# A fused attention layer: the tensor engine's program written out, two tiles moved between the sums, output buffers per chunk, and one PSUM bank moved from row scores to transposed scores

## The reference

```
xn = layernorm(x)                              # x: 2 x 2048 x 1024
q, k, v = xn @ wq, xn @ wk, xn @ wv            # 32 query heads, 8 key/value heads, width 32
scores = where(causal, q k^T * 32**-0.5, min)  # four query heads share one key/value head
s = (softmax(scores) @ v) @ wo
base = xn @ W_base.T + b_base
lora = sum over the top 2 of 8 experts of w_e * (xn @ A_e^T) @ B_e^T * 2
out = x + s * silu(base + lora)
```

## Time and profile before

| | |
|---|---|
| time, median of 3 runs | 3578.84 us (3575.22 to 3588.54) |
| the profiled execution: its own time / its span | 3588.89 us / 3587.1 us |
| PE busy, in all | 3328.6 us, 93% of the span |
| stretch of `attend` in which all five engines run | about 720 to 2820 us |
| mean granted clock of PE | 0.957 |

### The profile page before, as it was taken

How to read it: one execution, slowest core, us unless ns; L and a number is a source line. 1 busy time by engine, 2 the same in 40 slices (tenths; PEclk the granted TensorE clock), 3 DMA queues, 4 the chain that set the end, 5 groups by cost and what they waited for, 6 DMA issues and landing times. The chain is left out here.

```text
span 3587.1 us, 59110 instructions
## 1 busy us (share of the span) xinstructions
PE 3328.6 (93%) x17920; PEld 2219.9 (62%) x17920; DVE 1889.7 (53%) x4622; ACT 1443.8 (40%) x2658; POOL 1371.6 (38%) x565
## 2 busy tenths in 40 slices
PE   6999999799989988989999998999999699999999
PEld 5888888554545544544554554554554488877887
DVE  5333332676666666766766666676673222223333
ACT  3122121165655555655655555565565210100100
POOL 0000000075665665766766675676577100000000
PEclk9999999699999999999999999999999899999999
DMA  6555544356556556656656655655565454435554
GB/s 223 160 163 180 160 153 135 89 125 130 128 122 135 126 119 138 135 122 133 141 119 136 135 125 121 139 130 121 130 153 130 138 172 137 133 126 190 193 190 172
DMA packets 285847, 511.84 MB, mean 143 GB/s; under 512 B 41120, under 2 KB 156832, under 8 KB 263584
## 3 DMA queue, kind: packets, MB, share of 16 engines
q1 hardware_dynamic: 260256, 333.04, 31.5%
q0 software_dynamic: 23040, 167.78, 23.2%
q10 hardware_dynamic: 2304, 7.87, 0.6%
HBM read 205.03 MB, written 134.74 MB: 95 GB/s over the span
## 5 line engine op out<-in xcount | busy, mean ns | idle before, releaser
L890 POOL TENSOR_TENSOR added<-added,probs 128x2048 f32<-128x2048 f32 (+3 forms) x320 | 1182.5, 3695 | 806.8 <-PE o_ps L961 772.5
L1067 DVE TENSOR_REDUCE row_max<-rows_ps 128x1 f32<-128x512 f32 x1536 | 996.3, 683 | 417.6 <-PE rows_ps L923 415.9
L1043 ACT ACTIVATE probs<-cols_ps 128x512 f32<-128x512 f32 x1728 | 921.7, 609 | 324.1 <-PE cols_ps L1005 296.9
L1071 DVE CUSTOM_DVE_ANT_0 masked_rows<-rows_ps,tri 128x128 bf16<-128x128 f32 (+3 forms) x1024 | 485.0, 482 | 228.3 <-PE rows_ps L923 225.3
L1005 PE MATMUL cols_ps<-q_st,k_st 97*128 97x512 f32 x1248 | 530.3, 432 | 54.7 <-ACT dma_added L1043 54.1
L923 PE MATMUL rows_ps<-k_st,q_st 96*128 96x512 f32 (+3 forms) x1536 | 536.5, 382 | 24.7 <-DMA q_st<-scratch_q_hi 16.9
L961 PE MATMUL o_ps<-probs,v_st 128*32 128x512 f32 (+3 forms) x4224 | 434.1, 528 | 0.0
L1005 PE MATMUL cols_ps<-q_st_last,k_st 97*128 97x512 f32 x928 | 388.7, 433 | 34.5 <-issue 30.3
L1005 PEld LDWEIGHTS cols_ps<-q_st,k_st 97*128 97x128 f32 x1248 | 242.0, 194 | 225.6 <-issue 106.9
L923 PE MATMUL rows_ps<-k_st,q_st_last 96*128 96x512 f32 (+3 forms) x1024 | 373.8, 390 | 1.9
L923 PEld LDWEIGHTS rows_ps<-k_st,q_st 96*128 96x128 f32 x1536 | 302.5, 198 | 116.9 <-DVE row_max L1067 49.2
(11 more groups left out here) (113 smaller groups left out, 3912.3 us busy)
## 6 DMA issues: line engine op xcount, KB each, us to landing
dma_added<-probs POOLq DMA_DIRECT2D x160, 1024.0 KB, 7.7
q_st<-scratch_q_hi SPq DMA_DIRECT2D x96, 256.0 KB, 6.9
x_sb<-in_x SPq DMA_DIRECT2D x32, 512.0 KB, 4.0
scratch_xt_hi<-xt_hi SPq DMA_DIRECT2D x32, 512.0 KB, 6.1
scratch_xt_lo<-xt_lo SPq DMA_DIRECT2D x32, 512.0 KB, 6.8
scratch_q_hi<-out_hi SPq DMA_DIRECT2D x64, 256.0 KB, 2.4
scratch_q_lo<-out_lo SPq DMA_DIRECT2D x64, 256.0 KB, 2.9
l_sb<-scratch_l_inv SPq DMA_DIRECT2D x256, 64.0 KB, 5.0
```

Of the source, the lines that this page charges most:

```text
L890: nc.gpsimd.tensor_tensor(total[:, :, q0:CH], total[:, :, q0:CH], probs_of(c, j)[:, :, q0:CH], ALU.add).then_inc(pool_added, 1)
L1043: nc.scalar.activation(probs_of(c, j)[:, :, i * P:(i + 1) * P], cols_ps[cols_slot(AT_T[t])][:, :].rearrange("p (h q) -> p h q", h=NREP), A ...
L1067: nc.vector.tensor_reduce(into, bank[:, :], AX.X, ALU.max).then_inc(rows_free, 1)
L1071: nc.vector.tensor_tensor_reduce(masked_rows[rows_slot(k)][:, 0:keys], bank[:, 0:keys], tri[:, CH - keys:CH], 1.0, MASKED, ALU.add, ALU.ma ...
```

## The change

`NROWS` goes from 4 to 3 and `NCOLS` from 3 to 4. In chunk 3 key tile 11 is added by POOL instead of by a DMA, and key tile 12 is no longer added by POOL but left to the product with ones. `o_sb` and its semaphore `o_stored` are there four times, one for each chunk; ACT's copy to `l_sb` (Y) now waits for POOL's product that read that `l_sb` buffer two chunks earlier, instead of for the store of `o_sb`. PE's program goes through `over_stages_once`, which leaves the rows of a group after the last one out.

```diff
-NROWS, NCOLS, NPROBS = 4, 3, 11
+NROWS, NCOLS, NPROBS = 3, 4, 11
...
-ADDS = [[0, 1, 2, 3], [0, 3, 5, 6, 7], [0, 3, 5, 6, 8, 9, 10, 11], [0, 3, 5, 6, 8, 10, 12]]
-DMA_ADDS = [[], [1, 2, 4], [1, 2, 4, 7], [1, 2, 4, 7, 9, 11]]
-REST = [[], [], [], [13, 14, 15]]
+ADDS = [[0, 1, 2, 3], [0, 3, 5, 6, 7], [0, 3, 5, 6, 8, 9, 10, 11], [0, 3, 5, 6, 8, 10, 11]]
+DMA_ADDS = [[], [1, 2, 4], [1, 2, 4, 7], [1, 2, 4, 7, 9]]
+REST = [[], [], [], [12, 13, 14, 15]]
...
-        o_sb = [sb(f"o_sb{i}", [P, CH]) for i in range(2)]
+        o_sb = [sb(f"o_sb{i}", [P, CH]) for i in range(CPB)]
...
-        o_stored = [sem(f"a_o_stored{i}") for i in range(2)]
+        o_stored = [sem(f"a_o_stored{i}") for i in range(CPB)]
...   (over_stages_once)
-                    run(Step(g // 2, g % 2), c, [op for op in STAGES[c] if not (g == 0 and of_group_before(op))])
+                    run(Step(g // 2, g % 2), c, [op for op in STAGES[c]
+                                                   if not (g == 0 and of_group_before(op) or g == NG - 1 and of_group_after(op))])
...   (SP, L4)
-                                         o_sb[par][:, :]).then_inc(o_stored[par], 16)
+                                         o_sb[cc][:, :]).then_inc(o_stored[cc], 16)
...   (POOL, N)
-                        nc.gpsimd.tensor_tensor(o_sb[cc % 2][:, :], o_sb[cc % 2][:, :], l_sb[cc % 2][:, :], ALU.mult) \
+                        nc.gpsimd.tensor_tensor(o_sb[cc][:, :], o_sb[cc][:, :], l_sb[cc % 2][:, :], ALU.mult) \
...   (PE)
-            over_stages(pe, run)
+            over_stages_once(run)
...   (ACT, Y)
-                        act.wait_ge(o_stored[cc % 2], n.lin(32, 16 * (cc // 2) + 16 - 32 * back))
+                        if cc >= 2 or not (first_group(n) or n.lin(1, -back) == 0):
+                            act.wait_ge(norm_ready, n.lin(CPB, cc - 1 - CPB * back))
...   (ACT, O)
-                        act.wait_ge(o_stored[cc % 2], n.lin(32, 16 * (cc // 2) + 16 - 32 * back))
+                        act.wait_ge(o_stored[cc], n.lin(16, 16 - 16 * back))
                         act.wait_ge(values_done, n.lin(NVG, J_OFF[cc + 1] // PER_VISIT - back * NVG))
-                        nc.scalar.activation(o_sb[cc % 2][:, :], o_ps[:, :], ACT.Copy).then_inc(chunk_copied, 1)
+                        nc.scalar.activation(o_sb[cc][:, :], o_ps[:, :], ACT.Copy).then_inc(chunk_copied, 1)
```

More of the change, by code:

```diff
@@ L873, in run @@
                             sp.dma_start(dst[bass.ds(n.lin(1, -back), 1), :, cc * CH:(cc + 1) * CH].squeeze(0),
-                                         o_sb[par][:, :]).then_inc(o_stored[par], 16)
+                                         o_sb[cc][:, :]).then_inc(o_stored[cc], 16)
             over_stages(sp, run)
-            for s in range(2):
-                sp.wait_ge(o_stored[s], 16 + 16 * (CPB * NG // 2))
+            for s in range(CPB):
+                sp.wait_ge(o_stored[s], 16 + 16 * NG)
             sp.wait_ge(gw_loaded, 16 * NW)
```

## The result

The changed kernel takes 3526.43 us (median of 4 runs, 3520.26 to 3533.10), against 3580.36 us (4 runs) before. The ratio is 0.9848, 95% interval 0.9821 to 0.9874: 54 us less, where 77 had been worked out.

A forecast was written before the change was run, and what follows sets the result against it. The prediction took attention to be bound by PE, with three repeated stalls and slow-clock tails. Terms -94 - 77.5 - 21 - 5 + 14 + 103 + 5 = -75.5 us gave 3503 us at the median, range 3435 to 3570.

The forecast's parts named there:

- O and Y: PE's stalls from ACT's output-store wait (chunk 2's beginning) and tile 11's DMA addition (chunk 3) vanish: gains 94 and 77.5 us.
- the ones: Leaving tile 12 to the product with ones adds eight matmul records in 16 groups on PE's path: 14 us cost.
- the term for POOL in chunk 2: POOL, close behind PE at chunk 2's l_sb copy, holds it little, row waits giving most back: cost 5 us, 0 to 42.
- The loop: Writing out PE's program removes its six taken-branch stalls, but DVE's branch then partly holds PE: gain 21 us, 0 to 44.
- The row bank: With three row banks PE's row matmuls wait for DVE in 248 of 310 stretches: cost 103 us, 50 to 212.
- Rival (a): Row banks cost little, delays mostly falling into waits for ACT or POOL: 50 us cost, 3439 us in all; chance 0.17.
- The column bank: A fourth column bank removes PE's short waits for ACT: gain 5 us, 0 to 25.
- (b): POOL becomes the bound in chunk 2: 37 us more, 3540 us; chance 0.12.
- (c): Slower: each stretch of rows ends with a full DVE row's delay, 212 us instead of 103, 3612 us; chance 0.09.
- (d): PE's clock falls with many short waits, half clock for a fifth of the stretch: 197 us more, 3700 us; chance 0.04.
- (e): Unrolling PE does nothing, DVE's branch holding it the whole 5 us: 21 us more, 3524 us; chance 0.58 including the forecast.

## Why the prediction held, and where its working failed

The time lies in the range, 23 us above the value. That it came so near is in part luck: two errors of the working, 66 and 43 us, have opposite signs (see "The sum"). With only the one or only the other put right the value would have been 3569 or 3460, still inside the range. Step by step, with the measured price as a difference of medians:

- **O and Y.** Worked out at 94 and 77.5 us, less 14 for the ones and 5 for POOL: 152 us together. The run with the buffers and the sums alone (PE a loop, four row banks) is 101.5 us under the kernel before. Alone they gave 46 and 48 us, so these two add. The stalls went as described; the step that failed is the term for POOL in chunk 2. Its cost was put at 5 us, with 42 as its bound, by setting the row waits against it. Without those, POOL holds PE at Y for 31 us (4.4 of them in chunk 3 of the last group), with slow clock behind it: toward the upper bound. My estimate from that trace: 26 us more idle time than costed, 13 us by the clock behind it and some 5 us more at the branches are 44 of the missing 51. (The 198 us at half clock in the prediction leave out 13 us of a stretch that begins at 2807 us, in PE's wait behind `attend`; no term hangs on them.)
- **The loop.** Worked out at 21 us; 6 us (13 by each one's own kernel before) in the company of the other two edits. The mechanism (DVE's branch is laid bare) is shown by PE's waits for L1074 in the run with four row banks, 1.8 to 4.0 us at the six branches. In the changed kernel PE's pause there is 0.3 to 1.4 us, where 1.9 had been worked out. The gain was put too large.
- **The row bank.** Worked out at 103 us; 105.5 us where little else holds PE, 55 in the changed kernel, and 15 us *gained* in the kernel before. The working was right for the bare price, and the sum was wrong to take it whole: the prediction put POOL's cost at nearly nothing because of the row waits, which is to say that the row waits cost less by that much, and the same holds for DVE's branch. I charged the row bank in full and gave no credit for the 31 us of POOL, the 21 us of DVE's branch and their slow clock, most of which it spares. Rival (a) named this ("mostly fall into waits for ACT or POOL") and was half right.
- **The column bank.** 5 us worked out, 0 measured.
- **The sum.** -152, -21 and +98 were worked out (the last is the banks with the column bank's 5 us off); -101.5, -6 and +55 were measured. The first two errors are 66 us too much gain, the third is 43 us too much cost. Both come from POOL and DVE standing close behind PE, so they partly cancel; the prediction did not see this.
- **Rivals.** (b) is the bound in the runs with four row banks, not in the changed kernel, where L979 waits 12 us in all and 7.1 of them in chunk 3 of the last group. (c) would need 0.58 us a stretch; the clean price is 105.5/310 = 0.34. (d) falls: the clock is 0.99 with short waits in 248 stretches. The Trainium skill (TensorE: Matmul & The Clock Gate, "A second HAM failure mode: psum-queue depth-cycling") tells of a kernel whose short idle times between PSUM banks made the clock swing. In the changed kernel little of this is seen: 46 of the 2031 us of `attend` are at half clock (204 before), and 17 of these have no idle time over 0.6 us near them. (e) is near the truth for the loop.

So the change as a whole gives 54 us; without its bank swap it would have given 109 (3471 us), or 114 by that run's own kernel before.

## What to carry to other kernels

A wait's price holds only for the kernel that it is measured in. The two edits that removed stalls at different places added (46 and 48 us alone, 101.5 together); writing out PE's program gave 58 us alone and 6 to 13 beside them; and a slowdown ahead of a chain of DMAs was free, even a gain. To price a buffer, first remove what stands right behind it, or try both sizes again after the last other edit. And where records overlap, count the time from start to start: nearly nine tenths of the row bank's cost never showed as idle time. A table of waits should reach to the end of the stage: the last group, which has nothing behind it, holds the longest wait in several of these runs.

## What the runs showed of the hardware

**What slows an accumulating DMA: loads ahead of it by 4 us, an instruction fetch by 1.** An addition of 1 MB by one DMA on POOL's queue lands after 6.9 us (median) when no fetch and little else runs beside it (35 of the 160 in the kernel before). With over 140 packets of queue 1, the loads and stores that SP issues, it is 7.7 us (45 cases); with a packet of queue 8, 16 KB and 1.0 us long, 7.5 (14); with both 8.5 (29). With packets of queues 8, 14 and 1 it is 12.2 (22 cases, 7.3 to 14.0), but the long ones of these are not made by the fetches. This is an addition of tile 11 in the kernel before with only PE written out (1206.5 to 1218.4 us), without a packet of queue 8:

```profile
q1 hardware_dynamic: 598, 1.62, 55.2%
q0 software_dynamic: 144, 1.05, 44.6%
q14 instruction: 1, 0.01, 0.2%
...
dma_added<-probs POOLq DMA_DIRECT2D x1, 1024.0 KB, 11.9
```

What decides is whether the addition is issued ahead of SP's loads for the next group, which begin with `q_st_last`. Two additions of tile 11 in the kernel before, the first landing after 12.2 us, the second after 8.5:

```profile
2010.96 0.34 SPq L798 DMA_DIRECT2D q_st_last<-scratch_q_hi  x1
...
2011.89 0.88 POOL L900 DMA_DIRECT2D dma_added<-probs  x1 [1.95 <-DMA dma_added<-probs]
...
1489.12 0.88 POOL L900 DMA_DIRECT2D dma_added<-probs  x1 [2.00 <-ACT probs L1043]
...
1490.43 0.34 SPq L798 DMA_DIRECT2D q_st_last<-scratch_q_hi  x1
```

Four of the kernels add tile 11 by a DMA: the kernel before, and the three with only the banks, PE's program or the buffers changed. In 34 of their groups the first of these loads was issued before the addition or within 0.5 us behind it, and the addition took 10.0 to 14.0 us. In 26 groups it was issued 0.8 us or more behind it, and the addition took 7.9 to 9.5. (The last group of each has no such loads.) The loads follow PE: they are issued 10 us before PE comes to Y. So an addition that is issued 1 us later can land 4 us later.

The fetches move that race. Queue 8 carries PE's program, by its counts: 137 packets before and 113 in the changed kernel, whose PE program needs no register instructions for its waits. Queue 14, with packets of 8 KB, kept its 110 there and fell to 82 with DVE written out.

```profile
q8 instruction: 113, 1.85, 0.2%
q14 instruction: 110, 0.90, 0.1%
```

With PE written out 0.9 of the first four additions of a chunk 3 meet a packet of queue 8 on average, not 1.7, and each such meeting goes with 1.1 us more for the four (28.8, 29.9 and 31.1 us with none, one and two in that run). The last addition was then issued too late in 6 groups of 15, not in 12, and so the wait at Y fell from 56 to 19 us. All this is inferred from these cases; no run changed a fetch or the place of the loads alone.

**A wait of PE costs more than itself.** After a row matmul that waited for DVE the next tile mostly starts 0.33 us later and not 0.24. Over all tiles behind rows this is 50 us more than before, about as much as the added waiting itself (60 us). The weight loads show why. Usually a row's weights are loaded while the matmul ahead of it runs, 0.23 us before its own start (754 cases in the changed kernel). In 454 cases, those with the 0.33 us, the row's weight load starts only when the wait is over, together with its matmul; the tile's load follows 0.11 us later, and the tile starts 0.23 us behind its load, as ever. The weight loads of the stretch above:

```profile
1842.75 0.19 PEld L924 LDWEIGHTS rows_ps<-k_st,q_st 96*128 96x128 f32 x1 [0.30 <-DVE row_max L1070]
...
1842.86 0.19 PEld L1006 LDWEIGHTS cols_ps<-q_st_last,k_st 97*128 97x128 f32 x1
```
